# A depthwise convolution of 16 taps shared by three engines: four taps go to POOL, seven stay on DVE, five on PE

## The reference, cut to what matters

```python
D_CONV = 16
zxbcdt = x @ W_in
z = zxbcdt[..., :D_INNER]
xBC = zxbcdt[..., D_INNER:D_INNER + CONV_DIM]          # 256 + 2 * 64 = 384 channels
kernel = conv_w.T[:, None, :]
xBC = jax.lax.conv_general_dilated(xBC, kernel, window_strides=(1,), padding=[(D_CONV - 1, 0)],
        dimension_numbers=('NWC', 'WIO', 'NWC'), feature_group_count=CONV_DIM) + conv_b
xBC = jax.nn.silu(xBC)
xs = xBC[..., :D_INNER].reshape(b, l, NHEADS, HEADDIM)
Bm = xBC[..., D_INNER:D_INNER + N_STATE]
Cm = xBC[..., D_INNER + N_STATE:]
...                                                    # the scan over time, gated by silu(z), normed, @ W_out
```

## Time and the profile before

| | |
|---|---|
| median of 3 runs | 2279.24 us |
| lowest and highest | 2276.68 and 2282.23 us |
| the profiled execution's own time | 2276.11 us |
| its span, first to last instruction | 2274.4 us |
| its mean granted clock of TensorE | 0.945 |

### The profile page before, as it was taken

How to read it: one execution, slowest core, us unless ns; L and a number is a source line. 1 busy time by engine, 2 the same in 40 slices (tenths; PEclk the granted TensorE clock), 3 DMA queues, 4 the chain that set the end, 5 groups by cost and what they waited for, 6 DMA issues and landing times.

```text
span 2274.4 us, 74250 instructions
## 1 busy us (share of the span) xinstructions
PE 2000.1 (88%) x31569; PEld 1323.4 (58%) x31675; DVE 1705.3 (75%) x3808; ACT 1001.4 (44%) x2827; POOL 458.8 (20%) x793
## 2 busy tenths in 40 slices
PE   7888888998886888787799999985999789999998
PEld 5555534444454555553567677763666456677776
DVE  3444489999965878787888888843999668888887
ACT  2333236566652121221455555542554445555555
POOL 2211000000000434335012122243432112121200
PEclk9999699999978899898899999996999999999999
DMA  2000000000010000000311111106553211111111
GB/s 61 4 3 4 1 1 1 1 1 1 1 38 17 2 3 2 3 3 2 111 48 44 44 44 44 39 4 128 107 108 73 65 40 44 39 44 44 44 57 37
DMA packets 76083, 77.35 MB, mean 34 GB/s; under 512 B 15756, under 2 KB 57060, under 8 KB 74180
## 3 DMA queue, kind: packets, MB, share of 16 engines
q1 hardware_dynamic: 71848, 70.11, 12.1%
q10 hardware_dynamic: 3904, 2.49, 0.4%
HBM read 60.09 MB, written 11.82 MB: 32 GB/s over the span
## 4 chain that ended last, share of the span: by engine, by line
PE 24%; DVE 18%; ACT 6%; issue 5%; DMA 1%; ACTq 1%; SPq 1%; POOL 1%; another core or an unknown queue 0%; POOLq 0%; DVEq 0%
PE B L85 23%; DVE work L2097 4%; DVE hr L2061 3%; DVE work L2105 3%; DVE work L107 2%; ACT hr L103 2%; ACT ltc L103 2%; ACTq L2384 1%; ACT catt L103 1%; DVE lth L107 1%; DVE lh L107 1%; DVE lpq L107 1%; ACT work L103 1%; DVE gr L1911 1%; DVE work L1471 1%
## 5 line engine op out<-in xcount | busy, mean ns | idle before, releaser
L85 PE MATMUL B<-gr,wres 128*128 128x512 f32 x1248 | 353.3, 411 | 16.4 <-DVE work L2105 10.2
L103 ACT ACTIVATE work<-B 128x512 f32<-128x512 f32 (+5 forms) x460 | 233.3, 524 | 124.4 <-PE B L85 69.3
L2147 POOL COPY G<-lh 128x32 f32<-128x32 f32 x256 | 148.2, 579 | 680.3 <-DVE lh L107 680.3
L85 PE MATMUL B<-work 128*128 128x128 bf16 (+3 forms) x1408 | 259.6, 312 | 28.3 <-ACT work L103 7.0
L85 PEld LDWEIGHTS B<-gr,wres 128*128 128x128 f32 x1248 | 214.2, 189 | 83.4 <-DVE work L2105 27.8
L103 ACT ACTIVATE hr<-work 128x512 fp32r<-128x512 f32 x272 | 172.9, 636 | 146.6 <-DVE work L2105 76.7
L85 PEld LDWEIGHTS B<-work 128*128 128x128 bf16 (+2 forms) x1408 | 141.3, 127 | 138.8 <-issue 79.5
L2061 DVE TENSOR_TENSOR hr<-work,hr 128x512 fp32r<-128x512 f32 x272 | 186.5, 686 | 8.1 <-ACT hr L103 6.6
L2097 DVE TENSOR_TENSOR work<-work 128x512 f32<-128x512 f32 x256 | 178.7, 698 | 14.0 <-ACT work L103 6.6
L107 DVE SCALAR_TENSOR_TENSOR work<-work,cw 128x512 f32<-128x512 f32 x240 | 179.2, 746 | 5.9
L85 PE MATMUL B<-hr,wres 128*128 128x512 f32 x624 | 177.9, 394 | 1.0 <-DVE hr L2061 1.0
(11 more groups left out here) (254 smaller groups left out, 3790.2 us busy)
## 6 DMA issues: line engine op xcount, KB each, us to landing
work<-wdr SPq DMA_DIRECT2D x128, 256.0 KB, 3.1
scr<-catt SPq DMA_DIRECT2D x144, 64.0 KB
work<-scr SPq DMA_DIRECT2D x16, 384.0 KB
work<-scr SPq DMA_DIRECT2D x16, 192.0 KB
catt<-in_L_ffn_ew SPq DMA_DIRECT2D x24, 128.0 KB, 2.4
work<-scr SPq DMA_DIRECT2D x16, 128.0 KB
out<-work SPq DMA_DIRECT2D x32, 64.0 KB, 2.2
work<-in_x ACTq DMA_DIRECT2D x2, 512.0 KB, 5.3
```

The costliest lines, as they stand in the source:

```text
L85: return e.matmul(out, lhsT, rhs, start=start, stop=stop, skip_group_check=True)
L103: return e.activation(out, in_, func, bias=bias, scale=scale)
L2147: e.tensor_copy(self.G[:, :, t], self.lh[:, t % 4, :]).then_inc(*inc("l.pool", "h", li, t))
```

## The change

NT goes from 6 to 5 and a new constant NP = 4 says how many taps are POOL's. Taps 0 to 4 are PE's. POOL multiplies the shifted input by the weights of taps 5 to 8 and sums the four products in a tile `cps` of its own (two of them, used in turn), with `cpt` as scratch. It starts when ACT's copy of the input is there, and when DVE has read the sum of the convolution two before. DVE waits for POOL's sum (`conv.pool`), adds it to acc (`conv.p`), and then adds taps 9 to 15. In the POOL program the X adds of the waves get `yield`s ahead of them, so that they stand among the convolutions in the order of the weave. `ts` and `stt` are the helpers named above.

```diff
          "L0_cond_C_z", "L0_cond_C_r", "L0_cond_C")
 EXPERTS = (("L0_ffn_kernel_gating_EDF", "L0_ffn_kernel_up_EDF", "L0_ffn_kernel_down_EFD"),
            ("L1_ffn_ew1", "L1_ffn_ew2", "L1_ffn_ew3"))
-NT = 6
+NT, NP = 5, 4
 COND2_LAG = 22
 MAMBA_DT_TURNS = 6
 MAMBA_UNIT_TURNS = ((8, 1, 1, 1), (22, 1, 1, 1))
@@ -546,6 +546,9 @@
             m |= {"xdt": ar(128, 256), "cbm": ar(128, 128), "y4": ar(128, 4, 256), "sq": self.area(c, [128, 256]),
                   "ss": ar(128, 4), "yT": ar(128, 2, 512), "tm": ar(128, 512)}
             self.mw.append(m)
+        self.cps = [self.area(c, [128, 512]) for _ in range(2)]
+        self.cpt = self.area(w, [128, 512])
+        assert w[1] <= 74 * 256 - 3 * NT * 128
 
     def mprep_load(self, e):
         I = self.I
@@ -754,9 +757,12 @@
                 if n:
                     silu(n - 1)
                 e.wait_ge(*at("conv.b", n))
-                for k in range(NT, 16):
-                    if k > NT:
-                        e.wait_ge(*at("conv.acc", n, k - 1))
+                e.wait_ge(*at("conv.pool", n))
+                e.tensor_tensor(self.cvb[u % 4][:, c, :], self.cvb[u % 4][:, c, :], self.cps[n % 2], ALU.add).then_inc(
+                    *inc("conv.p", n))
+                yield
+                for k in range(NT + NP, 16):
+                    e.wait_ge(*(at("conv.acc", n, k - 1) if k > NT + NP else at("conv.p", n)))
                     stt(e, acc, X[:, :, 1 + k:129 + k], self.cw[:, c, k:k + 1], acc, ALU.mult, ALU.add).then_inc(
                         *(inc("conv.acc", n, k) if k < 15 else inc("conv.acc", n)))
                     if (15 - k) % 3 == 0 and k < 15:
@@ -767,11 +773,34 @@
         yield
 
     def conv_pool(self, e):
-        e.wait_ge(*self.at("xt", 7))
+
+        at, inc = self.at, self.inc
+        e.wait_ge(*at("xt", 7))
         for x in self.XP:
-            e.memset(x[:, :, 0:16], 0.0).then_inc(*self.inc("conv.pad"))
-        return
-        yield
+            e.memset(x[:, :, 0:16], 0.0).then_inc(*inc("conv.pad"))
+        yield
+        n = 0
+        for u in range(8):
+            for c in range(3):
+                X, P, tmp = self.XP[n % 3], self.cps[n % 2], self.cpt
+                yield
+                e.wait_ge(*at("conv.x", n))
+                if n >= 2:
+                    e.wait_ge(*at("conv.p", n - 2))
+                for k in range(NT, NT + NP):
+                    to = P if k == NT else tmp
+                    ts(e, to.rearrange("p (b t) -> p b t", b=4), X[:, :, 1 + k:129 + k], self.cw[:, c, k:k + 1],
+                       ALU.mult).then_inc(*inc("conv.pt", n, k))
+                    e.wait_ge(*at("conv.pt", n, k))
+                    if k > NT:
+                        e.tensor_tensor(P, P, tmp, ALU.add).then_inc(
+                            *(inc("conv.ps", n, k) if k < NT + NP - 1 else inc("conv.pool", n)))
+                        if k < NT + NP - 1:
+                            e.wait_ge(*at("conv.ps", n, k))
+                for _ in range(3):
+                    yield
+                n += 1
+            yield
 
     def mamba_turns(self, wk, i):
         for _ in range(MAMBA_UNIT_TURNS[wk][i]):
@@ -1044,8 +1073,15 @@
             yield
 
     def mamba_pool(self, e, wk):
+
+        for _ in range(MAMBA_DT_TURNS + 7):
+            yield
         for i in range(4):
             ub = UNITS[wk + 2 * i]
+            for _ in self.mamba_turns(wk, i):
+                yield
+            for _ in range(24):
+                yield
             e.wait_ge(*self.at(f"mw{wk}.dve", "X", i))
             e.tensor_tensor(flat(self.X, ub), flat(self.X, ub), flat(self.G, ub), ALU.add).then_inc(
                 *self.inc(f"mw{wk}.pool", "X", i))
```

## The result

The changed kernel takes 2319.65 us in the median of 4 runs (2313.39 to 2323.22), the kernel before 2277.96 beside it. The ratio is 1.0178, with a 95% interval of 1.0149 to 1.0206: 1.8% slower, some 41 us. The forecast was 2366, or +87 us. The profiled execution of the changed kernel has a span of 2311.7 us, 37.3 more than before.

The account below looks back on a forecast made before the run. DVE's instruction order bounds the convolution stage, with PE close behind. Own work -40, collisions +112, start +7, clock +8 give +87 on the profiled execution, 2363, or 2366 as median of the runs; range 2305 to 2435.

Parts of the forecast that it names:

- The mechanism: Convolution stage: DVE's instruction order sets the pace; POOL's work and DVE instructions with both inputs in SBUF go one after the other.
- the first rival: Convolution stage: POOL's reads and DVE's taps don't exclude each other; 21 to 40 us faster, say 30, 2249; chance 9%.
- the signs named for the mechanism: Convolution stage: taps 1.1 to 1.4 us, product for E over 1.21, POOL's adds 1.7 or more, taps' window some 430 us.
- For a multiplication I take the same 0.30 off: 1.19.: POOL's products beside DVE's taps: each costs DVE 0.30 less than its 1.49 us, as for the add, so 1.19.
- 65 of 177 hidden: 23 convolutions cost DVE 177 us; 65 fall where DVE reads PSUM, takes reciprocals or idles, and cost nothing.
- the term: Collisions in 23 convolutions at 7.7 us each: 177, less 65 hidden, so +112 us.
- the 8 us of the clock: Convolution stage: PE's lower share lowers its granted clock, lengthening answers DVE waits for; +8 us, bounds 0 and 25.
- the forecast's own case: Whole kernel, collisions at the predicted prices: 2323 to 2415 us around 2366; chance 62%.
- The third rival: POOL's multiplication takes only 0.61 us, costing DVE 0.31; 4.15 a convolution, 46 of 95 us hidden, +16, 2295; chance 10%.
- DVE's own work: Convolution stage: DVE loses three taps a convolution (57 us) and gains one add (17 us); -40, to 281 us.
- The start: Convolution 0: POOL's part runs beside the dt polynomial on DVE, so the first tap comes about 7 us later.
- order and waits: Convolution stage: the experiments' rival to collisions, no chance given; the prediction counted no wait, with about 4 us margin.

## Why the prediction was off

**The mechanism was right.** DVE bounds the stage before and after, the taps are longer while instructions with a PSUM operand are not, everything behind the stage is only shifted, and POOL's sum is in time. Leaving POOL's work out gives 34 us less, within the 21 to 40 that the first rival had for a kernel without collisions, and the add costs 0.9 to 1.0 us as read from one pair of instructions of the trace before (0.97). Of the signs named for the mechanism, the product for E is longer (1427 ns) and instructions with a PSUM operand are unchanged; those that hung on the size were missed: taps of 1.1 to 1.4 us (1.03), POOL's adds at 1.7 or more (1.46), 430 us from first to last tap (375).

**The step that failed** is this one: "For a multiplication I take the same 0.30 off: 1.19." Measured it is 0.31 to 0.42. I carried a rule from an instruction with two inputs (blocked nearly as long as it lasts) to one with one input that lasts longer. The multiplication's duration was well sized (1.49 forecast, 1.56 alone), but the duration doesn't set the price: the product of half the length costs DVE the same. An add reads two inputs of 512 elements, a product one; the trace before had no one-input instruction of POOL beside a two-input one of DVE at that size, and I named the whole duration as the upper bound of this price and did not put the weight on the lower side. The Trainium skill, SBUF — State Buffer, Who interferes with whom, has the pair held for the whole instruction; for a product of 1.56 us the runs show 0.31 to 0.42, so the measurement decides against it.

**What follows for the sum.** A convolution costs 4 x 0.31 + 3 x 0.97 = 4.15 us instead of 7.7, and 23 of them 95 instead of 177. I had 65 of 177 hidden, 37%, DVE's idle time included; measured are 68 us lost of 95, and less idle time took up 5 of these 68, so 34% is hidden. With the measured price and my share hidden the term is 60 instead of 112 and the sum +35 (-40 + 60 + 7 + 8); the profiled execution shows +37. That the two are so near is in part luck, since the 8 us of the clock stand for other things (below). And that 2320 lies between 2305 and 2435 is no merit of the working: the forecast's own case began at 2323. The third rival ("cheap multiplication", 2295) had the same 4.15 for another reason, a multiplication of 0.61 us, and hid 46 of 95: too much.

**The other terms.** DVE's own work: -40 forecast, 281 us left, and 280.5 measured with POOL idle. The start: 7 forecast, 7.4 measured in the dt chain, and the run with the late start shows that waiting doesn't save it, since POOL's first sum then comes later instead. The clock: the granted clock in the window is 0.92 against 0.97, and yet DVE waits only some 2 us for PE's products; my 8 us for it are not seen. In the sum they are made up for by 2.5 us ahead of and 3 behind the stage, which I had not forecast.

**The rival** that the time comes from order and waits is out with the run in which POOL is idle; the rival without collisions is out with the taps at 1032 ns.

## What to carry to other kernels

Work given to POOL isn't free for DVE when both sides work out of SBUF: count, for each POOL instruction, the SBUF inputs that it reads and not how long it lasts, here 0.3 to 0.4 us for one input of 512 and 0.9 to 1.0 for two, paid by a DVE instruction with two SBUF inputs that meets it. In this kernel POOL's share of a tap (75 us for 96 taps, so 0.78 each) costs as much time as the tap of 0.79 on DVE that it takes away, and DVE's add of POOL's sum costs 0.70 a convolution on top. A DVE chain that keeps its running sum in PSUM avoids the collision, but then the bank has to be free, and a price from one kind of instruction shouldn't be carried to another without a row for it.

## What was new of the hardware

- POOL's `tensor_scalar` 128x512 in 32-bit floats takes 1.56 us with one operation and 0.69 to 0.76 with two (multiply, then add 0 or a column). A tap that meets either loses 0.2 to 0.4 us, and an add of 1.26 us costs it 0.9 to 1.0.
- Writing alone, POOL leaves DVE's two-input instructions as they are (165 of 168 taps at 0.65 to 0.75 us, `tensor_tensor` 128x256 at 0.42) and lengthens DVE's `tensor_scalar` of 128x256 from SBUF to SBUF from 0.29 to 0.70 us each in the dt chain.
- What DVE loses to POOL in separate kernels doesn't add up (17.5 and 33 us against 75 together), since both draw on the same idle time and since POOL, at work for longer, is met more often.
